# A small vision tower on one core: transposes written to both partition halves by TensorE, and products of high parts ahead of the wait for low parts

## The reference

```python
h = tok(x)                       # 15-channel shifted 16x16 patches, layernorm, @ w: [8, 64, 192]
h = h + attn(layernorm(h))       # 12 heads; key j is seen by query i if j%8==0 and j<=i, or j in (i, i-1)
h = h + ffn(layernorm(h))        # 8 experts of 192 -> 768 -> 192, exact gelu, the two best of 8 per token

def ffn(flat):
    probs = softmax(flat @ router_w.T)
    top_w, top_i = top_k(probs, 2); top_w /= top_w.sum(-1)
    for e in range(8):
        w_e = sum(top_w * (top_i == e), -1)
        out += w_e * (gelu(flat @ w1[e] + b1[e]) @ w2[e] + b2[e])
```

## Time and profile before

| | us |
|---|---|
| median of 3 runs | 192.36 (192.32 to 192.62) |
| profiled execution | 192.19 |
| its span | 190.5 |
| TensorE busy | 170.2 (89%) |
| VectorE busy | 140.1 (74%) |
| ScalarE busy | 115.6 (61%) |
| GpSimd busy | 80.4 (42%) |

### The profile page before, as it was taken

How to read it: one execution, slowest core, us unless ns; L and a number is a source line. 1 busy time by engine, 2 the same in 40 slices (tenths; PEclk the granted TensorE clock), 3 DMA queues, 4 the chain that set the end, 5 groups by cost and what they waited for, 6 DMA issues and landing times.

```text
span 190.5 us, 3455 instructions
## 1 busy us (share of the span) xinstructions
PE 170.2 (89%) x1132; PEld 148.1 (78%) x1132; DVE 140.1 (74%) x319; ACT 115.6 (61%) x206; POOL 80.4 (42%) x103
## 2 busy tenths in 40 slices
PE   0598699988989776999999999999999999999994
PEld 0486549966768555779999999999899899899994
DVE  5389994498466875598759769858878788788653
ACT  2398643652634353665695795795796786874730
POOL 7875001131498511970335345354462662660000
PEclk9999999999999999999999999999999999999999
DMA  5999999400012930027001902803604600000002
GB/s 120 227 316 315 252 217 234 92 0 2 21 42 101 292 87 3 0 82 209 0 3 16 249 24 54 232 5 97 192 0 121 168 2 0 0 3 0 0 0 83
DMA packets 14691, 18.38 MB, mean 96 GB/s; under 512 B 2435, under 2 KB 10744, under 8 KB 14678
## 3 DMA queue, kind: packets, MB, share of 16 engines
q1 hardware_dynamic: 14134, 18.19, 36.0%
q10 hardware_dynamic: 544, 0.03, 0.2%
HBM read 17.44 MB, written 0.39 MB: 94 GB/s over the span
## 4 chain that ended last, share of the span: by engine, by line
PE 59%; DVE 6%; POOL 3%; issue 1%; ACT 1%; POOLq 0%; DVEq 0%
PE ps L371 30%; PE ps L1138 17%; PE ps L1140 8%; DVE big_r L1213 3%; PE ps L1182 1%; PE ps L1181 1%; PE ps L1180 1%; POOL h L559 1%; POOL halo L567 1%; DVE merge L1213 1%; POOL wsplit L329 1%; ACT big_r L333 1%; POOL halo L572 1%; DVE shifted L1213 0%; PE ps L945 0%
## 5 line engine op out<-in xcount | busy, mean ns | idle before, releaser
L371 PE MATMUL ps<-big_r,wsplit 128*128 128x512 f32 (+1 forms) x255 | 62.8, 382 | 0.0
L757 ACT ACTIVATE early<-ps,b1t 128x512 f32<-128x512 f32 x48 | 32.8, 684 | 29.8 <-PE ps L371 29.8
L1138 PE MATMUL ps<-wsplit,big_r 128*128 128x384 f32 x168 | 49.7, 355 | 0.7 <-DVE big_r L1213 0.7
L1213 DVE TENSOR_TENSOR big_r<-early,big_r 128x512 fp32r<-128x512 f32 x48 | 38.3, 802 | 16.1 <-ACT big_r L333 15.7
L371 PEld LDWEIGHTS ps<-big_r,wsplit 128*128 128x128 f32 x255 | 43.1, 188 | 6.4
L1140 PE MATMUL ps<-wsplit,big_r 128*128 128x192 f32 x168 | 42.1, 250 | 0.0
L1138 PEld LDWEIGHTS ps<-wsplit,big_r 128*128 128x128 f32 x168 | 31.5, 188 | 3.0 <-DVE big_r L1213 0.9
L1140 PEld LDWEIGHTS ps<-wsplit,big_r 128*128 128x128 f32 x168 | 32.0, 190 | 1.3
L333 ACT ACTIVATE big_r<-early 128x512 fp32r<-128x512 f32 x48 | 30.4, 633 | 1.5
L1549 DVE SCALAR_TENSOR_TENSOR merge<-sq,gates,merge 128x192 f32<-128x192 f32 x32 | 26.9, 865 | 0.0
L315 POOL TENSOR_TENSOR wsplit<-stage,wsplit 128x768 fp32r<-128x768 f32 x4 | 7.4, 1850 | 19.5 <-ACT wsplit L333 15.9
(11 more groups left out here) (226 smaller groups left out, 273.3 us busy)
## 6 DMA issues: line engine op xcount, KB each, us to landing
stage<-in_L_ffn_w SPq DMA_DIRECT2D x4, 576.0 KB, 6.5
early<-in_L_ffn_w SPq DMA_DIRECT2D x4, 576.0 KB, 6.0
shifted<-in_L_tok_w SPq DMA_DIRECT2D x6, 288.0 KB, 8.9
early<-in_x SPq DMA_DIRECT2D x3, 512.0 KB, 6.7
stage<-in_L_ffn_w SPq DMA_DIRECT2D x4, 384.0 KB, 4.1
stage<-in_L_ffn_w SPq DMA_DIRECT2D x8, 192.0 KB, 5.2
early<-in_L_ffn_w SPq DMA_DIRECT2D x4, 384.0 KB, 3.2
early<-in_L_ffn_w SPq DMA_DIRECT2D x8, 192.0 KB, 4.1
```

Of the source, the lines that this page charges most:

```text
L371: mm = nc.tensor.matmul(dst, lhs, rhs, start=(first and n == 0), stop=(last and n == 4))
L757: nc.scalar.activation(gf[:, j % NG], ps[:, HPB[j % 4], :], ACT.Gelu, bias=b1t[:, bass.ds(k, 1)]).then_inc(s_gelu, 1)
L1138: nc.tensor.matmul(ps[:, AB[t], 0:2 * D], g_hi[:, j % NG, tok], w2c, start=(f == 0), stop=False)
L1213: return nc.vector.tensor_tensor(o, a, b, op)
```

## The change

It has four parts. `last_columns_again` and the like copy of `ao` are gone from ScalarE, with their semaphores. `transposes` makes the second half of a tile in two steps on TensorE, each from the 64 columns themselves: a transpose onto partitions 0 to 63 and a plain fp32 matmul with the identity onto partitions 64 to 127. The five products are split into `high_products` (three, which need high parts of the tokens alone) and `low_products` (two): for the first q and k products of group 0, for the first token tile of each `projection`, and for the router and the first hidden chunk of both groups of the second layernorm, the high ones are issued between the wait for the high part and the wait for the low part. Last, GpSimd's `split_low_w2` of the second expert is moved behind the power of the gates and waits for VectorE's second low part of a hidden chunk (`s_glo` 2).

```diff
+        def high_products(dst, x_of, w_of, x_stationary=False, first=True):
+            for n, (a, b) in enumerate(((0, 0), (0, 1), (2, 2))):
+                lhs, rhs = (x_of(a), w_of(b)) if x_stationary else (w_of(b), x_of(a))
+                nc.tensor.matmul(dst, lhs, rhs, start=(first and n == 0), stop=False)
+
+        def low_products(dst, x_of, w_of, x_stationary=False, last=True):
+            for n, (a, b) in enumerate(((1, 0), (3, 2))):
+                lhs, rhs = (x_of(a), w_of(b)) if x_stationary else (w_of(b), x_of(a))
+                mm = nc.tensor.matmul(dst, lhs, rhs, start=False, stop=(last and n == 1))
+            return mm
...
             pool.wait_ge(s_n2lo, G)
-            split_low(pool, 1, 1)
+            split_low_w1(pool, 1, 1)
             pool.wait_ge(c_euler, 1)
             pool.wait_ge(s_gsub, 1)
             nc.gpsimd.tensor_tensor(gs[:, 1], euler[:], gs[:, 0], ALU.pow).then_inc(s_gexp, 1)
+            pool.wait_ge(s_glo, 2)
+            split_low_w2(pool, 1, 1)
...
-            def last_columns_again(which, g, dst):
-                for t in (2 * g, 2 * g + 1):
-                    act.wait_ge(s_n, which * TT + t + 1)
-                    copy(dst[:, t, D:], dst[:, t, P:D]).then_inc(s_ndup, 1)
...
-                act.wait_ge(s_ao, g + 1)
-                copy(ao[:, 2 * g:2 * g + 2, D:], ao[:, 2 * g:2 * g + 2, P:D]).then_inc(s_aodup, 1)
                 high_parts(g, s_at, ATB, aot, s_ahi)
...
-                for r in range(2):
-                    for n in range(2):
-                        t = 2 * g + n
-                        if r == 0:
-                            pe.wait_ge(ready, count(t))
-                        elif again:
-                            pe.wait_ge(again, count(t))
-                        mm = nc.tensor.transpose(ps[:, banks[g], r * TG + n * P:r * TG + (n + 1) * P],
-                                                 src[:, t, r * P:(r + 1) * P], ident)
+                for n in range(2):
+                    t = 2 * g + n
+                    pe.wait_ge(ready, count(t))
+                    nc.tensor.transpose(ps[:, banks[g], n * P:(n + 1) * P], src[:, t, 0:P], ident)
+                for n in range(2):
+                    nc.tensor.transpose(ps[0:REM, banks[g], TG + n * P:TG + (n + 1) * P], src[:, 2 * g + n, P:D], ident)
+                    mm = nc.tensor.matmul(ps[REM:P, banks[g], TG + n * P:TG + (n + 1) * P], src[:, 2 * g + n, P:D], ident,
+                                          start=True, stop=True)
                 mm.then_inc(done, 1)
...
                 pe.wait_ge(s_ahi, g + 1)
+                high_products(ps[:, OB[g], 0:D], lambda a: aot[:, a, own[0]], w, True)
                 pe.wait_ge(s_alo, g + 1)
-                for n in range(2):
-                    tok = slice((2 * g + n) * P, (2 * g + n + 1) * P)
-                    mm = triple(ps[:, OB[g], n * D:(n + 1) * D], lambda a: aot[:, a, tok],
-                                wx_(slice(OUT0, OUT0 + D)), True)
-                mm.then_inc(s_op, 1)
+                low_products(ps[:, OB[g], 0:D], lambda a: aot[:, a, own[0]], w, True)
+                triple(ps[:, OB[g], D:2 * D], lambda a: aot[:, a, own[1]], w, True).then_inc(s_op, 1)
...
             pe.wait_ge(s_nhi, 1)
+            high_products(ps[:, QB[0], 0:TG], nx(first_half), wx_(slice(0, P)))
+            high_products(ps[:, KB[0], 0:TG], nx(first_half), wx_(slice(D, D + P)))
             pe.wait_ge(s_nlo, 1)
...
                 pe.wait_ge(s_n2hi, g + 1)
+                router = ps[0:E, RB, cols], lambda a: n2t[:, a, cols], wx_(slice(ROUT0, ROUT0 + E))
+                chunk0 = ps[:, HPB[0], cols], router[1], lambda b: wsplit[0][:, offs[b]:offs[b] + P]
+                high_products(*router)
+                high_products(*chunk0)
                 pe.wait_ge(s_n2lo, g + 1)
```

More of the change, by code:

```diff
@@ L226, in vit_tower @@
         s_t1, s_t2, s_h = (sem(n) for n in ("s_t1", "s_t2", "s_h"))
-        s_bn, s_mv, s_ve, s_rs, s_n, s_ndup = (sem(n) for n in ("s_bn", "s_mv", "s_ve", "s_rs", "s_n", "s_ndup"))
+        s_bn, s_mv, s_ve, s_rs, s_n = (sem(n) for n in ("s_bn", "s_mv", "s_ve", "s_rs", "s_n"))
         s_nt, s_nhi, s_nlo = (sem(n) for n in ("s_nt", "s_nhi", "s_nlo"))
@@ L235, in vit_tower @@
             sem(n) for n in ("s_mask", "s_maskx", "s_prod", "s_nearps", "s_nearsb", "s_sps", "s_mx", "s_sub", "s_exp", "s_rden"))
[L236 to L237 removed]
+        s_ptps, s_pt, s_pv, s_nvp, s_nv, s_pvn, s_ao = (
+            sem(n) for n in ("s_ptps", "s_pt", "s_pv", "s_nvp", "s_nv", "s_pvn", "s_ao"))
         s_vbias, s_row, s_hrow, s_at, s_ahi, s_alo, s_op, s_h2 = (
@@ L933, in _, with transposes @@
             small_transposes(3)
-            def transposes(g, src, ready, count, banks, done, again=None):
-                for r in range(2):
-                    for n in range(2):
-                        t = 2 * g + n
-                        if r == 0:
-                            pe.wait_ge(ready, count(t))
-                        elif again:
-                            pe.wait_ge(again, count(t))
-                        mm = nc.tensor.transpose(ps[:, banks[g], r * TG + n * P:r * TG + (n + 1) * P],
-                                                 src[:, t, r * P:(r + 1) * P], ident)
+            def transposes(g, src, ready, count, banks, done):
+                for n in range(2):
[6 more added lines that the diff above has]
+                                          start=True, stop=True)
                 mm.then_inc(done, 1)
@@ L1044, in projection @@
             def projection(g):
+                own = [slice((2 * g + n) * P, (2 * g + n + 1) * P) for n in range(2)]
+                w = wx_(slice(OUT0, OUT0 + D))
                 pe.wait_ge(s_ahi, g + 1)
+                high_products(ps[:, OB[g], 0:D], lambda a: aot[:, a, own[0]], w, True)
                 pe.wait_ge(s_alo, g + 1)
-                for n in range(2):
-                    tok = slice((2 * g + n) * P, (2 * g + n + 1) * P)
-                    mm = triple(ps[:, OB[g], n * D:(n + 1) * D], lambda a: aot[:, a, tok],
-                                wx_(slice(OUT0, OUT0 + D)), True)
-                mm.then_inc(s_op, 1)
+                low_products(ps[:, OB[g], 0:D], lambda a: aot[:, a, own[0]], w, True)
+                triple(ps[:, OB[g], D:2 * D], lambda a: aot[:, a, own[1]], w, True).then_inc(s_op, 1)
             pe.wait_ge(s_meansq, 1)
@@ L1063, in _ @@
                 nc.tensor.matmul(ps[:, NTB[0], :], xh[:, 0, 0:P], xh[:, 0, :], start=True, stop=True)
-            transposes(0, n1, s_n, lambda t: t + 1, NTB, s_nt, s_ndup)
+            transposes(0, n1, s_n, lambda t: t + 1, NTB, s_nt)
             pe.wait_ge(s_watlo, 4)
@@ L1103, in _ @@
             transposed_p(1)
-            transposes(0, ao, s_ao, lambda t: t // 2 + 1, ATB, s_at, s_aodup)
+            transposes(0, ao, s_ao, lambda t: t // 2 + 1, ATB, s_at)
             strided_values(1)
@@ L1107, in _ @@
             pe.wait_ge(s_vbd, TT)
-            transposes(1, ao, s_ao, lambda t: t // 2 + 1, ATB, s_at, s_aodup)
+            transposes(1, ao, s_ao, lambda t: t // 2 + 1, ATB, s_at)
             keep_busy(3)
@@ L1145, in _ @@
             pe.wait_ge(s_w1lo, 1)
-            transposes(0, n2, s_n, lambda t: TT + t + 1, N2B, s_n2t, s_ndup)
+            transposes(0, n2, s_n, lambda t: TT + t + 1, N2B, s_n2t)
             for g in range(G):
@@ L1149, in _ @@
                 pe.wait_ge(s_n2hi, g + 1)
+                router = ps[0:E, RB, cols], lambda a: n2t[:, a, cols], wx_(slice(ROUT0, ROUT0 + E))
+                chunk0 = ps[:, HPB[0], cols], router[1], lambda b: wsplit[0][:, offs[b]:offs[b] + P]
+                high_products(*router)
+                high_products(*chunk0)
                 pe.wait_ge(s_n2lo, g + 1)
-                triple(ps[0:E, RB, cols], lambda a: n2t[:, a, cols], wx_(slice(ROUT0, ROUT0 + E)), False)\
-                    .then_inc(s_rl, 1)
-                for j in range(EARLY):
+                low_products(*router).then_inc(s_rl, 1)
+                mm = low_products(*chunk0)
+                if g == 1:
+                    mm.then_inc(s_mm1, 1)
+                for j in range(1, EARLY):
                     if (g, j) == (0, 1):
-                        transposes(1, n2, s_n, lambda t: TT + t + 1, N2B, s_n2t, s_ndup)
+                        transposes(1, n2, s_n, lambda t: TT + t + 1, N2B, s_n2t)
                     mm = triple(ps[:, HPB[j], cols], lambda a: n2t[:, a, cols],
```

14 lines of the change are left out of this document (6 added, 8 removed).

## The result

The changed kernel takes 194.84 us (median of 9 runs), the kernel before 192.62 us beside it (9 runs): a ratio of 1.0084, 95% interval 1.0056 to 1.0113, so 1.1 to 2.2 us slower. The ratio leaves out one slow execution of the changed kernel, 196.56 us, over 1.5% above its fastest. The forecast was 191.2 us with a range of 190.4 to 192.4. The sign was wrong, and the rival called "slower than before" is nearest to what came. The profiled execution took 194.84 us, span 193.1.

The account below looks back on a forecast made before the run. The experts' gapless TensorE block could only start earlier, set by the low/high-part chain and GpSimd's splits; -1.2 us there plus 0.05 at the scores gave -1.15, so 192.36 became 191.2 us, range 190.4 to 192.4.

Parts of the forecast that it names:

- slower than before: Rival: mixed groups run record after record with drains, 1.34 us each; sum +0.35 to +0.8, 192.7 to 193.2 us; chance 0.13.
- What bounds the kernel: TensorE has no gap from 84 us, so the experts' block can only start earlier; the low/high-part chain decides when.
- The group: New transpose group: halves side by side and one change, +0.32 us on the old 0.60, so 0.92 us.
- upper end of 1.34: Group's upper bound: all eight records in sequence, +0.44 us, and three changes between halves and whole array, +0.30.
- three and a half: Places where longer groups are paid: scores, first attention output group, both groups of the second layernorm.
- Before the attention output: Early q and k products bring no gain; longer second transposes first eat 0.24 us spare at the scores.
- The attention output: Two groups: three products each run before the low part, second group's transposes cost nothing; -0.63 us at 70.2.
- The second layernorm: Longer groups cost +0.32, six products move ahead of each low part; first hidden chunk and everything after on TensorE -1.03.
- The moved split: At the experts: second low part no longer stands; comparisons and third low part stand instead; third block -1.4 to -1.0, taken -1.2.
- The sign that was to speak against standing: Evidence for cheaper rival (chance 0.09): VectorE's 128x4 operation began during GpSimd's split at 78.04, took its usual 0.17 us.
- The sum: -1.2 us at the experts plus 0.05 for the scores: -1.15 us, giving 191.2 us.
- the wall that was to hold the third block at 84.9: VectorE's comparisons and third low part stand behind the moved split, so the third block starts at 84.7 to 85.1.

Follow-up runs that it names:

- halves_plain: Changed kernel with both 64-column halves written by plain fp32 matmuls with the identity, lower and upper in turn; ratio to the kernel before 0.9973 (0.9948 to 0.9998).
- halves_together: Changed kernel with each group sorted: full transposes, both 64-column transposes, then both plain matmuls; ratio to the kernel before 0.9986 (0.9955 to 1.0016).
- only_high: Kernel before with only the high-part products moved ahead of the low-part wait; ratio to the kernel before 0.9928 (0.9898 to 0.9958).
- only_split: Kernel before with only the second expert's split_low_w2 moved behind the power; ratio to the kernel before 0.9970 (0.9937 to 1.0004).
- low_first: old_transposes with VectorE's first low part of a hidden chunk ahead of the gates' maxima; ratio to the kernel before 0.9935 (0.9904 to 0.9967).
- old_transposes: Changed kernel with the old transposes and ScalarE's copies back; ratio to the kernel before 0.9878 (0.9842 to 0.9914).

## Why the prediction was wrong, step by step

**What bounds the kernel: right.** The experts only shift; the 102.08 or 102.09 us behind the fourth block is the same in every profile.

**The group, the step that failed.** It was put at 0.92 us "because L1040 is the nearest row". L1040's matmuls are all plain, on both halves; the new group's lower half is a transpose. halves_plain has the pair that L1040 has, and there the group is 0.96 us, what was forecast. With the transpose in it there is nothing side by side, and the group is 1.44 us, above the upper end of 1.34. The parts of that upper end were nearly right: eight records, three changes at 0.10 (0.20 to 0.23 against 0.109 between the records), and on top 0.05 us more in each pair of plain records (0.160 instead of 0.109). The rule quoted beside the choice, from the Trainium skill, TensorEngine Tiling (Array Packing), Restrictions, that column tiling excludes transpose mode for fp32 input, agrees with this: the transposes on 64 columns behave as full-width work (0.109 us to and from full transposes), and only the plain ones as work on half an array. Its other rule, under Key Properties, that a change of mode drains TensorE, agrees as far as these changes cost 0.10 us. A small output alone is no such change: products of 64 columns onto the lower half in TensorE's fast form (fp32r; L371, 53.04 to 53.51 us before) and the router's 8 columns follow and precede full-width ones at 0.12 us. Two rules against one row should have had more than 0.13, all the more as the row differed from the case in just the point that one of the rules names.

**What a group costs was also too small.** The forecast counted the group inside. Leaving it costs as well: in halves_together's second group the next product starts 0.20 us behind the last plain record and the one after it 0.22, where behind a transpose they start 0.03 and 0.20 later. The trace of before had this too: behind L1040 each of L978's first two records comes 0.26 us behind the record ahead of it, where 0.163 is usual, and the forecast counted one. And it was paid at more places than three and a half. By the distances, the changed kernel against halves_plain is 2.31 us for 0.48 us a group, 4.8 groups' worth:

| from the first transposes, against before, us | changed kernel | halves_plain | only_high |
|---|---|---|---|
| second group of the first layernorm | +0.30 | 0.00 | -0.01 |
| first group of the attention output | +0.58 | -0.19 | -0.01 |
| second group of the attention output | +1.14 | +0.19 | -0.12 |
| first group of the second layernorm | +1.17 | -0.24 | -0.79 |
| second group of the second layernorm | +1.22 | -0.66 | -1.58 |
| first product block | +2.04 | -0.30 | -1.48 |
| second product block | +1.43 | -0.92 | -1.47 |
| fourth product block | +1.38 | -0.93 | -1.47 |

**Before the attention output.** That the early products of q and k bring nothing was right (-0.01 in only_high). The 0.24 us of spare time at the scores was eaten first, as said, and the scores' sum came 0.95 us later. Half of that was given back by an order that nobody planned. Before, VectorE's next product (`merge`, 61.78) begins 0.22 us behind GpSimd's product of the next scores and takes 1.06 us. In the changed kernel and in halves_plain it begins 0.11 us ahead of it and takes 0.56. In return GpSimd's product starts later (0.50 us in halves_plain), and that delays the second group of the output. This is why halves_plain has -0.19 in one row of the table and +0.19 in the next.

**The attention output.** Forecast -0.63 with a group of 0.92. only_high, with the old group, gains 0.78 from the first group of the output to the first of the second layernorm, so the gain of the high products was sized well. But with the group at 0.96 (halves_plain) only 0.05 us of it is left there. Part of that is the exchange just described, the rest the longer groups; how much each takes isn't separated. That the second group's transposes sit beside VectorE's work and "cost nothing" fell with their length: VectorE waited 0.59 us at 70.91.

**The second layernorm.** Between its first group and the first product block only_high gains 0.69 us. The forecast had -0.40 for TensorE there, with longer groups, and held the first block at -0.8 in all because VectorE would get to the low part late. In the changed kernel this stretch loses 0.87 us.

**The moved split.** Forecast: a wait of 0.6 us goes at the second block. Measured: 0.60 in only_split (+0.03 to -0.57), and 0.61 in the changed kernel. What stands behind the split was named by kind, not by name: the comparisons were expected to, but the cast of 128x32 ahead of them did, 2.35 us where it takes 0.18. The third block stayed in step (2.29 us behind the second), with the third low part done only about 0.1 us ahead of it. low_first shows what happens when that 0.1 us is gone. The sign that was to speak against standing, a 128x4 operation that took 0.17 us at 79.80 before, ended 0.10 us behind the end of GpSimd's split, so it had hardly anything to wait for. In old_transposes it meets the split earlier, takes 0.59 us and ends 0.03 us behind it. The Trainium skill, SBUF — State Buffer, under SBUF: two separate sides, says that VectorE and GpSimd share one pair of ports, that a VectorE operation in one of its two-port modes or with two SBUF inputs needs it, and that the loser waits for the whole instruction. The low part, the comparison and the 128x4 subtraction have two SBUF inputs and agree (1.97, 2.57 and 0.59 us). The cast and the addition of a constant to `gs` have one and stood too (2.35 and 2.66 us); whether they ran in a two-port mode no trace tells. One row doesn't agree: beside GpSimd's power of the gates (1.30 us at 83.46 in the changed kernel) VectorE's second low part, with two SBUF inputs, kept its 0.68 us.

**The sum.** With the group at 0.96 us (halves_plain, whose first transposes start at 41.34 us, so that the times compare directly) the change gives -0.93 by distance (the ratio says 0.04 to 1.0 us faster), where -1.15 was forecast for 0.92. That it came so near is partly luck, since on the way it was further off and the misses offset each other: the first block came at 80.38, not 79.9, and the second at 82.76, not 82.3, since the longer groups cost more than booked; but the wall that was to hold the third block at 84.9 didn't bind, and it came at 85.05. The price of the group as it was written turned the -0.93 into +1.38. A group over 1.2 us had been named as the sign of a wrong forecast. The rival "slower" had the mechanism and the sign, and with +0.35 to +0.8 a size too small, for the two reasons above.

## What to carry to other kernels

The halves of TensorE's array overlapped here where both sides were plain matmuls; in this kernel a transpose in the pair undid it and each change cost 0.10 us, so the group that mixed them was longer than one that did more work of one kind. When the nearest row is not the same form as the new instruction, price the sum by both ends and ask which of them the difference in form speaks for. A big GpSimd operation was a wall for small VectorE ones: place it by what is queued behind the first thing that hits it, and look at the last margin (here 0.1 us), since moving anything ahead can use it up.

## What the runs showed of the hardware

- Plain fp32 matmuls of 64 columns onto the lower and the upper half ran side by side: eight records in 0.66 us. Coming to them from full-width work costs 0.20 us instead of 0.109 between records, going back 0.20 and 0.22 for the next two products, where behind a transpose it is 0.03 and 0.20.
- A 64-column fp32 transpose onto the lower half follows and precedes full-width transposes and plain full-width matmuls at 0.109 to 0.112 us, with no price for the change. Nor did products of 64 columns onto the lower half alone have one in the fast form, fp32r (0.12 us). A plain fp32 one on the lower half alone, and transposes on both halves, weren't tried.
- A cast of 128x32, an addition of a constant to 128x4 and a comparison of 128x32 each stood for the length of a GpSimd operation of 128x1152 (2.35, 2.66 and 2.57 us). It goes both ways: where VectorE's `merge` began 0.11 us ahead of it, GpSimd's product of 128x384 took 1.18 us instead of 0.87. A low part with one input in PSUM didn't stand (0.69 us).
- TensorE's clock came up at 10.3 to 13.6 us in nine profiles and at 18.4 to 19.3 us in four, with the same matmuls ahead of it; the first transposes come about 1.2 us later in the latter. In the changed kernel TensorE had a matmul in flight in all of the 12.00 to 18.00 us at the lower level. What decides it is open.
